# Attention probabilities of one layer computed for all batches ahead of its stage, and kept in DRAM

## What is computed

```python
def _L3_xattn_ref(teacher_logits, teacher_features, Wq, bq, Wk, bk):
    query = jnp.einsum('bnc,dc->bnd', teacher_features, Wq) + bq
    key = jnp.einsum('bnc,dc->bnd', teacher_features, Wk) + bk
    energy = jnp.einsum('bnd,bmd->bnm', query, key)
    attention = jax.nn.softmax(energy, axis=-1)
    return jnp.einsum('bln,bmn->blm', teacher_logits, attention)

x = x + tanh(g_xattn[0]) * ssm(ctx, layernorm(x))                # s0
x = x + tanh(g_ffn[0])   * mixture_of_experts(layernorm(x))      # s1
x = x + tanh(g_xattn[1]) * smoothquant_int8(layernorm(x), ctx)   # s2
x = x + tanh(g_ffn[1])   * ternary_swiglu(layernorm(x))          # s3
x = x + tanh(g_xattn[2]) * cross_attention(layernorm(x), ctx)    # s4, sa
x = x + tanh(g_ffn[2])   * eight_bit_swiglu(layernorm(x))        # s5
x = x + tanh(g_xattn[3]) * _L3_xattn_ref(layernorm(x), ctx, ...) # s6
x = x + tanh(g_ffn[3])   * group_ternary_swiglu(layernorm(x))    # s7
```

## Time and profile before

| what | us |
|---|---|
| median of three runs | 1066.01 |
| the profiled run, as a whole | 1062.76 |
| its span (what the trace covers) | 1061.0 |
| PE matmul busy | 860.5 |
| PE weight loads busy | 616.9 |
| DVE busy | 723.4 |
| ACT busy | 531.3 |
| POOL busy | 278.6 |

### The profile page before, as it was taken

The page is one execution under the profiler, slowest core; times in us unless marked ns, Lnnn a source line. Parts: engine busy times, 40 slices in busy tenths (PEclk is TensorE's granted clock), DMA queues, the critical chain, the costliest instruction groups (busy, mean ns, idle before and its releaser), DMA issues.

```text
span 1061.0 us, 13347 instructions
## 1 busy us (share of the span) xinstructions
PE 860.5 (81%) x4120; PEld 616.9 (58%) x4120; DVE 723.4 (68%) x1780; ACT 531.3 (50%) x1254; POOL 278.6 (26%) x365
## 2 busy tenths in 40 slices
PE   2888997865899987678888789979999779697465
PEld 1445655534557865545776567558776647475244
DVE  3897789785547876885789876774568763355632
ACT  8777874312464544536635445653355544464313
POOL 1200021201334310550584013415310433200305
PEclk9999999986999998989999999989999989799557
DMA  6675455435532221341263134404411243110102
GB/s 232 218 252 194 144 179 163 144 122 171 155 104 99 83 77 55 85 154 51 76 195 96 43 96 139 149 16 136 134 52 57 75 124 118 43 40 21 30 1 70
DMA packets 56615, 116.54 MB, mean 110 GB/s; under 512 B 6232, under 2 KB 18400, under 8 KB 55392
## 3 DMA queue, kind: packets, MB, share of 16 engines
q1 hardware_dynamic: 47328, 90.51, 26.7%
q0 software_dynamic: 9216, 25.17, 8.4%
HBM read 97.74 MB, written 17.92 MB: 109 GB/s over the span
## 4 chain that ended last, share of the span: by engine, by line
PE 44%; DVE 22%; issue 16%; POOL 10%; ACT 6%; DMA 1%; SPq 1%; POOLq 0%; DVEq 0%; ACTq 0%
PE bk L1318 28%; PE bk L1397 6%; PE bk L1634 2%; PE bk L1606 2%; DVE ssm_u L1943 2%; POOL aclB L922 2%; PE bk L1382 2%; POOL arA L902 2%; POOL arB L928 1%; POOL ring L993 1%; DVE ssm_u L1937 1%; DVE mx L2161 1%; PE bk L1390 1%; POOL aclA L922 1%; DVE lnbuf L1848 1%
## 5 line engine op out<-in xcount | busy, mean ns | idle before, releaser
L1318 PE MATMUL bk<-hTA,ringT 128*128 128x256 f32 x448 | 110.6, 393 | 0.0
L856 POOL TENSOR_TENSOR lnbuf<-lnbuf,mhalf 128x2 f32<-128x2 f32 x32 | 24.3, 759 | 309.5 <-DVE lnbuf L1854 309.5
L1318 PEld LDWEIGHTS bk<-hTA,ringT 128*128 128x128 f32 x448 | 87.6, 198 | 14.6 <-issue 2.3
L1318 PE MATMUL bk<-qk 128*128 128x256 f32 x288 | 81.6, 410 | 4.1 <-ACT arB L1209 2.3
L1209 ACT ACTIVATE arB<-bk,nb,rqs 128x256 f32<-128x256 f32 x128 | 71.0, 561 | 24.6 <-DVE nb L2164 24.2
L1943 DVE TENSOR_TENSOR_SCAN ssm_u<-ssm_da,ssm_u 128x512 f32<-128x512 f32 x64 | 79.6, 1244 | 3.4 <-issue 0.3
L1318 PE MATMUL bk<-arB,cx 128*128 128x256 f32 x256 | 73.0, 410 | 10.7 <-DVE qk L2200 6.8
L902 POOL TENSOR_TENSOR arA<-t2A,arA 128x256 f32<-128x256 f32 x44 | 38.6, 878 | 125.9 <-DVE t2A L1976 125.6
L1127 ACT ACTIVATE ssm_da<-sdl,nega 128x255 f32<-128x255 f32 x128 | 56.8, 500 | 24.1 <-DVE ssm_u L1943 24.0
L1243 ACT ACTIVATE arB<-bk 128x512 f32<-128x512 f32 x64 | 38.2, 597 | 60.4 <-PE bk L1606 60.1
L1318 PEld LDWEIGHTS bk<-qk 128*128 128x128 f32 x288 | 55.7, 204 | 20.6 <-issue 9.8
(11 more groups left out here) (338 smaller groups left out, 2178.3 us busy)
## 6 DMA issues: line engine op xcount, KB each, us to landing
ringT<-in_w SPq DMA_DIRECT2D x56, 384.0 KB, 3.3
ringQ<-in_wqk SPq DMA_DIRECT2D x40, 384.0 KB, 3.1
ring<-q3s POOLq DMA_DIRECT2D x32, 384.0 KB, 3.4
ring<-q7s POOLq DMA_DIRECT2D x32, 384.0 KB, 3.5
qk<-kTs SPq DMA_DIRECT2D x32, 256.0 KB, 4.4
ringM<-m4s SPq DMA_DIRECT2D x32, 256.0 KB, 3.2
kTs<-thB SPq DMA_DIRECT2D x11, 256.0 KB, 4.4
kTs<-t1B SPq DMA_DIRECT2D x11, 256.0 KB, 2.0
```

Of the source, the lines that this page charges most:

```text
L1318: return t_.matmul(dst, lhsT, rhs, start=start, stop=stop)
```

## The change

The probabilities of `s6` are made for all four batches in the preparation, by a new generator `probs6` on PE, ACT and DVE, which stands behind the keys' norms and ahead of the queries `s4` of batch 0. It works in bank `AR` and in the three tiles `kst`, and writes each batch's transposed probabilities to a DRAM tensor `p6s` (256 KB each, issued by SP). `load6` brings them back into `thB` in stage `s5`, once DVE's step `t1` 7 has read that tile for the last time. `s6` keeps the normalisation, its transpose, the final product and the residual. The eight DMAs are new; the arithmetic is the same in kind and number.

```diff
-        q6, e0 = cut(arB, 0, 2, S)
-        pm6, e0 = cut(arB, e0, 2, S)
-        pT6, e0 = cut(arB, e0, 2, S)
...
+        pT6, q6, pm6 = kst
...
         PLAN = {
...
-                    3: ((0, 2676.39), (3, 3098.80), (8, 3203.41),)},
...
+                    3: ((3, 3303.56), (8, 3455.87),)},
...
-                    yield at6(b - 3, AT6["qk"] + 0.5)
-                    sp.wait_ge(*at(b - 3, "s6.pe", "qk"))
+                    yield at0(b, -10)
+                    sp.wait_ge(*at(None, "k6.pe", "qk", b - 3))
+                    sp.wait_ge(*at(b - 3, "s2.dve", "x", 1))
...
+            def spill6():
+                for b in range(B):
+                    yield at_p6(12 * b + 11.5)
+                    sp.wait_ge(*at(None, "k6.act", "pT", b))
+                    sp.dma_start(a["p6s"][b], flat(pT6)).then_inc(dma_sem("p6s"), 16)
+            def load6(b):
+                yield place("p6l", 0, b)
+                if b == 0:
+                    sp.wait_ge(dma_sem("p6s"), 16 * B)
+                sp.wait_ge(*at(b, "s5.dve", "t1", 7))
+                sp.dma_start(flat(pT6), a["p6s"][b]).then_inc(dma_sem("p6l"), 16)
...
             def s6(b):
-                yield at6(b, AT6["qk"])
-                act.wait_ge(*at(b, "s6.pe", "qk"))
-                for j in range(2):
-                    s.activation(q6[:, j, :], OP[:, j * S:j * S + S], ACT.Identity, bias=b6[:, j:j + 1]).then_inc(*sig("s6.act", "qk", j))
                 yield at6(b, AT6["exp"])
-                softmax(b, "s6", 0, NH, SC, pm6, lambda t: 1.0)
                 evac_hT(b, "s6", hTB[:, :, :], PT)
-                yield at6(b, AT6["pt"])
-                act.wait_ge(*at(b, "s6.pe", "pt", 0))
-                s.activation(pT6, halves(OP), ACT.Copy).then_inc(*sig("s6.act", "pT", 0))
+            def probs6():
+                for b in range(B):
+                    yield at_p6(12 * b + 1)
+                    act.wait_ge(*at(None, "k6.pe", "qk", b))
+                    if b == 0:
+                        for i in range(3):
+                            act.wait_ge(dma_sem(f"ks{i}"), 16 * len(range(i, NK, 3)))
+                    for j in range(2):
+                        s.activation(q6[:, j, :], AR[:, j * S:j * S + S], ACT.Identity, bias=b6[:, j:j + 1]).then_inc(*sig("k6.act", "qk", b, j))
+                    yield at_p6(12 * b + 6)
+                    act.wait_ge(*at(None, "k6.dve", "nb", b))
+                    if b:
+                        act.wait_ge(*at(None, "k6.pe", "pt", b - 1))
+                    for t in range(2):
+                        s.activation(pm6[:, t, :], AR[:, t * S:t * S + S], ACT.Exp, bias=nb4[:, NH, t:t + 1],
+                                     accum_out=den4[:, NH, t:t + 1]).then_inc(*sig("k6.act", "ex", b, t))
+                    yield at_p6(12 * b + 10)
+                    act.wait_ge(*at(None, "k6.pe", "pt", b))
+                    if b:
+                        act.wait_ge(dma_sem("p6s"), 16 * b)
+                    s.activation(pT6, halves(AR), ACT.Copy).then_inc(*sig("k6.act", "pT", b))
...
+            def probs6():
+                for b in range(B):
+                    yield at_p6(12 * b)
+                    if b:
+                        pe.wait_ge(*at(None, "k6.act", "pT", b - 1))
+                    else:
+                        pe.wait_ge(*at(None, "k0.act", "ln"))
+                    for j in range(2):
+                        i = mm(half(AR, j), w6[:, j, :], cxK[b])
+                    i.then_inc(*sig("k6.pe", "qk", b))
+                    yield at_p6(12 * b + 3)
+                    pe.wait_ge(*at(None, "k6.act", "qk", b, 1))
+                    for t in range(2):
+                        i = mm(half(AR, t), q6[:, 0, t * P:t * P + P], q6[:, 1, :])
+                    i.then_inc(*sig("k6.pe", "sc", b))
+                    yield at_p6(12 * b + 8)
+                    for t in range(2):
+                        pe.wait_ge(*at(None, "k6.dve", "pn", b, t))
+                        for kc in range(2):
+                            i = t_.transpose(AR[:, kc * S + t * P:kc * S + t * P + P], pm6[:, t, kc * P:kc * P + P], ident[:, :])
+                    i.then_inc(*sig("k6.pe", "pt", b))
...
-                    pe.wait_ge(*at(None, "k0.act", "ln"))
+                    pe.wait_ge(*at(None, "k6.act", "pT", B - 1))
                     pe.wait_ge(*at(1, "sx.dve", "yg"))
                 transpose_h(b, "s4", h, bank)
...
             def s6(b):
-                yield at6(b, AT6["qk"])
-                for j in range(2):
-                    i = mm(half(OP, j), w6[:, j, :], cxTs[b % 3][:, :])
-                i.then_inc(*sig("s6.pe", "qk"))
                 yield at6(b, AT6["sc"])
-                pe.wait_ge(*at(b, "s6.act", "qk", 1))
-                for t in range(2):
-                    i = mm(half(SC, t), q6[:, 0, t * P:t * P + P], q6[:, 1, :])
-                i.then_inc(*sig("s6.pe", "sc", 0))
                 transpose_h(b, "s6", hB, PT)
                 yield at6(b, AT6["pt"])
-                probsT(b, "s6", 0, pm6, OP)
-                pe.wait_ge(*at(b, "s6.act", "pT", 0))
+                pe.wait_ge(*at(b, "s6.act", "hT"))
+                pe.wait_ge(dma_sem("p6l"), 16 * (b + 1))
                 for t in range(2):
                     for kc in range(2):
                         i = t_.matmul(half(AR, t), hTB[:, kc, t * P:t * P + P], pT6[:, kc, :],
...
+            def probs6():
+                K = "k6.dve"
+                for b in range(B):
+                    yield at_p6(12 * b + 4.5)
+                    dve.wait_ge(*at(None, "k6.pe", "sc", b))
+                    v.tensor_reduce(mx4[:, NH, :], halves(AR), AXX, ALU.max).then_inc(*sig(K, "mx", b))
+                    dve.wait_ge(*at(None, K, "mx", b))
+                    v.tensor_scalar(nb4[:, NH, :], mx4[:, NH, :], -1.0, None, ALU.mult).then_inc(*sig(K, "nb", b))
+                    yield at_p6(12 * b + 7)
+                    dve.wait_ge(*at(None, "k6.act", "ex", b, 1))
+                    v.reciprocal(rd4[:, NH, :], den4[:, NH, :]).then_inc(*sig(K, "rd", b))
+                    dve.wait_ge(*at(None, K, "rd", b))
+                    for t in range(2):
+                        v.tensor_scalar(pm6[:, t, :], pm6[:, t, :], rd4[:, NH, t:t + 1], None, ALU.mult).then_inc(*sig(K, "pn", b, t))
...
+                if b == 0:
+                    dve.wait_ge(dma_sem("p6s"), 16 * B)
...
-                yield at6(b, AT6["sc"] + 1)
-                smax(b, "s6", 0, NH, SC)
-                yield at6(b, AT6["exp"] + 1)
-                rden(b, "s6", 0, NH, pm6)
                 yield at6(b, AT6["x"])
                 dve.wait_ge(*at(b, "s6.pe", "dn"))
                 residual(b, "s6", AR, lambda t: tg[:, 3:4])
...
+        for n, c, w in (("q3s", NCF, SLOT), ("q7s", NCF, SLOT), ("m4s", NH // 2, 2 * D), ("kTs", B * NH // 2, 2 * S), ("p6s", B, 2 * S)):
```

More of the change, by code:

```diff
@@ new lines, in build @@
+                "state": {0: ((0, -19.74), (0.2, 448.77), (4, 458.80), (4.2, 458.81), (7, 468.83), (7.2, 468.84), (7.7, 472.91), (12, 483.07), (12.2, 503.48), (12.7, 834.79), (15, 928.40), (15.7, 928.41), (16, 1194.02), (17, 1195.13),),
[3 rows of a table added]
+                "ternary": {0: ((0.5, 19.97), (0.6, 39.78), (1.5, 415.90), (1.6, 427.81), (2.5, 436.00), (2.6, 448.25), (3.5, 457.74), (3.6, 459.99), (4.5, 466.17), (4.6, 469.80), (5.5, 478.00), (5.6, 743.56), (6, 826.37),)},
+                "w2": {0: ((0, 159.30), (1, 425.81),),
+                    1: ((0, 2179.70), (1, 2230.31),),
+                    2: ((0, 2526.85), (1, 2528.86),),
+                    3: ((0, 2999.25), (1, 3010.36),)},
@@ L809, in each @@
                     yield from stage(b)
[L811 removed]
+            interleave(each(load0), each(load1), each(fillT), fillK(), loadK(), loadR(), spill6(), each(load6), each(fillQ), each(fillM), prepare(), spill7(), spill4(), each(store))
             for b in range(B):
@@ L1308, in rest @@
                 yield from swiglu(b, "s7")
-            interleave(each(front), experts(), ternary(), group_ternary(), copy7(), value_output(), keys(), each(wide), each(middle), each(rest))
+            interleave(each(front), experts(), ternary(), group_ternary(), copy7(), value_output(), keys(), probs6(), each(wide), each(middle), each(rest))
         @block.tensor
@@ L1764, in rest @@
                 yield from swiglu(b, "s7")
-            interleave(each(front), ternary(), group_ternary(), value_output(), keys(), each(wide), each(middle), each(rest))
+            interleave(each(front), ternary(), group_ternary(), value_output(), keys(), probs6(), each(wide), each(middle), each(rest))
         @block.vector
@@ L2312, in rest @@
                 yield from swiglu(b, "s7")
-            interleave(each(front), ternary(), group_ternary(), norms_k(), each(middle), each(weights2), each(rest))
+            interleave(each(front), ternary(), group_ternary(), norms_k(), probs6(), each(middle), each(weights2), each(rest))
         return o.seen
```

87 lines of the change are left out of this document (36 added, 51 removed), and 393 rows, old and new, of the table PLAN.

## The result

| | before | after |
|---|---|---|
| median (four runs each) | 1066.36 us | 1079.64 us |
| profiled run, and its span | 1062.76, 1061.0 | 1077.69, 1075.9 |

What follows compares the result with a forecast made beforehand. The bound was taken to change: DVE and PE nearly full from 110 to 249 us, PE busiest to 914, one engine-to-engine chain from 1013. Front +8, middle −8, tail −4 gave −4: 1066.01 to 1062 us, range 1051 to 1073.

Steps and rivals of the forecast that it cites:

- Front, +8: Preparation and front up to batch 0's cross attention: added work and new order cost 8 us, bounds −8 and +15.
- 12 later and 4 given back: Batch 0's `s3` starts 12 us later; 4 return before its cross attention because preparation there was pulled ahead.
- the slower rival: Rival at 1072, chance 0.33; its sign was batch 0's cross attention starting 14 us or more later than 325.
- third sub-step: End of batch 0's `s2` stands behind batch 1's routing: `s3` later by 3.7 us plus batch 1's front delay.
- The added work, 7.2 us of DVE within the front: Probabilities of four batches, 110 to 325 us: DVE 7.2 us, ACT 10, PE some 4 each; could just fit or add.
- Middle, −8: Stages `s6` of batches 0 to 2: shorter waits there save 8 us, bounds −15 and 0.
- Tail, −3.9: `s6` of batch 3: final product starts 4.3 us after the residual instead of 8.2, saving 3.9, bounds −3 to −5.
- Load, 0: The 256 KB load from DRAM into `thB` costs nothing, covered by the down product of `s5`.
- The front is not given back: Rival: late `xpad`, keys and DVE work cost +14, middle and tail give 4 each: +6, 1072; chance 0.33.
- Nothing in the balance: Rival: work sets the middle, `s6` stalls were filled anyway; middle 0, front +4, tail −4: 1066; chance 0.14.

Runs made afterwards that it cites:

- two tables: Changed kernel without the probabilities' work, spills and loads, steps ahead of `s3` of batch 0 placed by the table before: 1058.25 us, ratio 0.995 against the kernel before.
- start of the keys: Changed kernel with products, copies and spills of the first three chunks of keys moved behind the start of `s0`: 1079.11 us, ratio 1.0162 against the kernel before.
- end of `s2`: Changed kernel with batch 0's last `s2` piece and `s3` beside the end of front 1, batch 1's routing behind that piece: 1071.9 us, ratio 1.0086 against before.
- start as before: Changed kernel with everything up to the end of front 0 in the order before, on all engines and SP: 1078.82 us, ratio 1.0141 against the kernel before.

## Why the prediction was wrong

Forecast 1062, measured 1079.64. By the traces the change is +14.9 instead of −4, and the runs split it: −6.6 for the work taken out of `s6` (the order before without the work), +17.6 for the new order (the same work left out under either table, +11.0 against −6.6), +3.9 for the added work (after against the work left out; 2.3 by the ratios). Of the 17.6, 15.8 hang on the table ahead of `s3` of batch 0 (+11.0 against −4.8 with two tables); the other 1.8 can't be told from none (0.9943 and 0.995).

- **Front, +8: wrong, and this is the step that failed.** I put it as "12 later and 4 given back", a middle value that no row gives. `s3` of batch 0 ends 17.2 later, and so does the cross attention of batch 0 (442.2 instead of 425.0): over the 14 that I had named for its start as the sign of the slower rival, with nothing given back. I looked for the cause at the start. `xpad` and the first scan came as forecast (20.78 and 51.35), but with before's start `s3` was 18.3 late all the same. Batch 0 itself had made its 8 us up: its `s1` ended 10.6 earlier than before, and the last product of `s2` was there at 244.8. Late was front 1, by 18.0, with before's start by 19.3, with before's table up to `s3` not at all; and the end of `s2` waited 18.7 us behind it. My third sub-step had the right form: 3.7 plus front 1's delay of 18 gives 21.7 for the end of `s2`, near the 19.7 measured. But I bounded that delay by what the start makes of it, and averaged the sum with hopes of giving back.
- **The added work, 7.2 us of DVE within the front: right in bounds.** 0.4 us at `s3` of batch 0, up to 3.9 at the end. In the order before, leaving it out takes 6.9 us off DVE's busy time (723.4 to 716.5), 9.2 off ACT's and 9.0 off PE's; I had 7.2, 10 and 16, since PE's durations came from the tail at a clock of 0.52. Of the 3.9, 2.0 come in `s6` of batch 0 (13.8 us long, 11.8 without the work), where the profiled run of after had a granted clock of 0.90. Three kernels with all the work and the same order there (start of the keys, end of `s2`, start as before) took 12.1 to 12.2 us, at 1.00. So most of the 2.0 is not the work's; that the clock made it is likely, not isolated.
- **Middle, −8: mis-sized.** −2.9 in `s6` of batch 0, zero in batches 1 and 2, even with before's order. In after, where I had forecast 2.6 less in batches 1 and 2, their `s6` is 0.0 and 1.0 shorter; the 1.0 is no effect of the change, as the same stage is 1.1 longer with the work left out. What batch 0 gains is lost around it (+17.2 at `s3` of batch 0, +18.1 at `s5` of batch 3). The row of PE's 1.0 idle us in 10 had it right: the final product keeps its place among other stages' work.
- **Tail, −3.9: right.** −3.8 in after and in the order before. 4.46 us from residual to product, predicted 4.3; the product again 3.79.
- **Load, 0: right.** Out 15.1 us ahead of the product.
- **The rivals.** "The front is not given back" (1072) is what happened, by a larger front and for another reason than the late `xpad`. "Nothing in the balance" fell in the result, and with it what I had read out of the Trainium skill in "Perfetto Trace Analysis", section "Identifying the Most-Contended Engine": that the change takes nothing off the busiest engine and so gives 1066. That section ranks engines by busy time, and busy time doesn't see what decided here: with the work left out, the two tables give the same 1760 instructions on DVE, busy for 727.1 and 716.5 us, and ends that are 17.6 us apart.

Open is why front 1 is late: which of the pieces that now stand ahead of its state steps, `s1` of batch 0, keys or group stage, cost how much. The 10.84 us of idle DVE were seen with the start as before, not isolated in after; a table with only these moved was not tried.
